# Lookahead and roots in the second attention layer, and a shared comparison in the first, of a graph and expert kernel

## The reference

```python
def _gat(x, src, dst, W, a_src, a_dst, b, heads, ch, concat):
    h = (x @ W).reshape(n, heads, ch)
    es, ed = (h * a_src).sum(-1), (h * a_dst).sum(-1)
    e = jax.nn.leaky_relu(es[src] + ed[dst], SLOPE)
    w = jnp.exp(e - jax.ops.segment_max(e, dst, num_segments=n)[dst])
    alpha = w / jax.ops.segment_sum(w, dst, num_segments=n)[dst]
    return jax.ops.segment_sum(h[src] * alpha[:, :, None], dst, num_segments=n) ... + b

x = x + gat2(relu(layernorm(gat1(layernorm(x)))))
x = x + experts(layernorm(x))     # router, top 2 of 8, gelu between two products
```

## Time and profile before

| | |
|---|---|
| time of three runs | 1572.95, 1572.9 and 1552.66 us |
| median | 1572.9 us |
| profiled execution | 1562.67 us |
| its span (first to last instruction) | 1560.7 us, granted TensorE clock 0.92 on the mean |
| busy in the span | PE 81%, PEld 61%, DVE 59%, ACT 46%, POOL 44% |

### The profile page before, as it was taken

How to read it: one execution, slowest core, us unless ns; L and a number is a source line. 1 busy time by engine, 2 the same in 40 slices (tenths; PEclk the granted TensorE clock), 3 DMA queues, 4 the chain that set the end, 5 groups by cost and what they waited for, 6 DMA issues and landing times.

```text
span 1560.7 us, 21436 instructions
## 1 busy us (share of the span) xinstructions
PE 1259.3 (81%) x6282; PEld 959.0 (61%) x6283; DVE 915.4 (59%) x2551; ACT 725.5 (46%) x1834; POOL 692.8 (44%) x626
## 2 busy tenths in 40 slices
PE   0767798979889989749778788873699999999990
PEld 0545354535445545337567577652699999999980
DVE  6769898999899987525555665667511111111115
ACT  0357665657656667425444544442034344335330
POOL 3600788656666671056565666520422222222220
PEclk9979899999999999869898999886699999999995
DMA  7012633623633470243443554422022222121116
GB/s 223 5 42 78 166 91 89 179 75 89 176 87 89 125 198 25 96 126 102 150 144 103 155 158 113 136 56 78 11 91 94 94 94 91 37 94 37 36 31 250
DMA packets 120379, 160.59 MB, mean 103 GB/s; under 512 B 53198, under 2 KB 93009, under 8 KB 120302
## 3 DMA queue, kind: packets, MB, share of 16 engines
q0 software_dynamic: 28384, 76.23, 17.9%
q1 hardware_dynamic: 86608, 78.89, 16.2%
q10 hardware_dynamic: 5310, 4.58, 0.9%
HBM read 124.98 MB, written 34.64 MB: 102 GB/s over the span
## 4 chain that ended last, share of the span: by engine, by line
PE 50%; DVE 26%; issue 8%; ACT 5%; DMA 4%; another core or an unknown queue 4%; ACTq 1%; SPq 1%; POOL 1%; DVEq 0%; POOLq 0%
PE bank L1381 13%; PE bank L1389 12%; PE bank L1263 9%; PE bank L1214 6%; DVE ring_a L1805 5%; PE bank L1335 4%; DVE ohk L1546 3%; ACT ring_a L1062 2%; DVE ohs L1543 2%; DVE st L1468 2%; PE bank L1123 1%; PE bank L1146 1%; DVE hit L1710 1%; PE bank L1246 1%
## 5 line engine op out<-in xcount | busy, mean ns | idle before, releaser
L750 POOL DMA_INDIRECT arena<-rows,idx_e x385 | 432.8, 1124 | 291.7 <-PE bank L1214 106.4
L1263 PE MATMUL bank<-ring_a,slots 128*65 128x384 f32 (+1 forms) x1000 | 343.9, 457 | 51.7 <-DVE ring_a L1805 45.0
L1335 PE MATMUL bank<-h2t,ring_a 128*128 128x257 f32 x650 | 186.2, 425 | 82.3 <-DVE ring_a L1880 59.3
L982 ACT ACTIVATE ring_a<-vbb,slots 128x384 f32<-128x384 f32 (+1 forms) x500 | 243.8, 562 | 15.4 <-DMA vbb<-v_rows 12.2
L1263 PEld LDWEIGHTS bank<-ring_a,slots 128*65 128x65 f32 x1000 | 136.1, 142 | 181.8 <-issue 101.2
L1805 DVE SCALAR_TENSOR_TENSOR ring_a<-ring_a,arena 128x1536 f32<-128x1536 f32 (+1 forms) x125 | 192.3, 1540 | 16.4 <-ACT ring_a L982 10.3
L1086 ACT ACTIVATE ring_a<-bank,cols 128x128 f32<-128x128 f32 x432 | 128.2, 370 | 158.0 <-PE bank L1381 157.2
L1335 PEld LDWEIGHTS bank<-h2t,ring_a 128*128 128x128 f32 x650 | 126.9, 207 | 116.3 <-DVE ring_a L1880 68.4
L1214 PE MATMUL bank<-arena,ring_a 128*128 128x257 f32 (+1 forms) x770 | 194.3, 402 | 0.0
L1214 PEld LDWEIGHTS bank<-arena,ring_a 128*128 128x128 f32 x770 | 157.4, 205 | 34.9 <-issue 5.4
L1880 DVE SCALAR_TENSOR_TENSOR ring_a<-ring_a,p,arena 128x256 f32<-128x256 f32 (+1 forms) x175 | 79.3, 464 | 114.9 <-ACT ring_a L1062 84.4
(11 more groups left out here) (277 smaller groups left out, 1721.9 us busy)
## 6 DMA issues: line engine op xcount, KB each, us to landing
counts_all<-arena SPq DMA_DIRECT2D x13, 800.0 KB
arena<-counts_all SPq DMA_DIRECT2D x13, 800.0 KB
arena<-in_L_ffn_W SPq DMA_DIRECT2D x8, 1024.0 KB, 7.5
arena<-rows,idx_e POOLq DMA_INDIRECT x385
arena<-ytab SPq DMA_DIRECT2D x4, 1280.0 KB, 11.0
XB<-general_sums SPq DMA_DIRECT2D x38, 130.0 KB
vbb<-in_L_ffn_W SPq DMA_DIRECT2D x4, 1024.0 KB
spare<-in_L_ffn_W SPq DMA_DIRECT2D x4, 1024.0 KB
```

The source lines that it names most:

```text
L750: pool.indirect_dma_start(to[:, k, 0:width], None, table, bass.IndirectOffsetOnAxis(idx_e[:, m * PAIR + k:m * PAIR + k + 1], 0)).then_inc( ...
L982: ins = act.activation(S1[q % SLOTS1][:, h * k * P:(h + 1) * k * P].rearrange("p (t n) -> p t n", n=P), vb1[:, 0:k, h, :], ACT.Copy, scale ...
L1263: pe.matmul(bank[h][0:CH + 1, 0:w_], slots[:, s, h * (CH + 1):(h + 1) * (CH + 1)], S1[q % SLOTS1][:, h * w_:(h + 1) * w_], start=(s == 0), ...
L1335: ins = pe.matmul(bank[(j % 2) * 2 + i][:, 0:W2T], S2[q2 % SLOTS2][:, i * P:(i + 1) * P], h2t[:, s, 0:W2T], start=(s == 0), stop=(s == NT ...
```

## The change

Layer 2, order: ScalarE and VectorE no longer do a step's product just ahead of the same step's other work. ScalarE's loop issues product m and then the other work of step m - 4 (`AHEAD_ACT`), VectorE's loop product m and then the other work of step m - 2 (`AHEAD_DVE`). TensorE, GpSimd and SyncE have the same order by step numbers.

Layer 2, roots: `root_of`, `ask_root` and `refine` are no longer called. `inverse_root` computes the inverse square root on VectorE from the bits of the number and three rounds of Newton, twice in a row for a group, all of it in the step of the group's last `norm`; `turn` comes earlier in the plan by 4 steps for a single tile standing alone.

Layer 1: the comparison is made once for all heads, 128x160 where it was 128x640, and laid out with the five edges innermost; the weights `W1` are laid out head, destination, edge, so that one broadcast over the heads serves. VectorE reads the exponentials of the gathered rows with edges innermost (neighbours 264 numbers apart), and TensorE's weight loads of a pair read every fifth number. In layer 2 the last product of a pair reads the comparison at every fifth number (line 1751).

```diff
+AHEAD_ACT, AHEAD_DVE = 4, 2
@@ plan2
-        g.root = g.norm[-1] + 1
-        g.refine = g.root + 1
+        g.refine = g.norm[-1]
...
-            turn = max(turn + 2, g.refine + 3)
+            turn = max(turn + 2, g.refine + 1)
@@ build
-        hit = sb("hit", [P, PAIR * HEADS * PW])
+        hit = sb("hit", [P, PW, PAIR])
@@ block.scalar
-                for k in range(2):
-                    for g in G2:
-                        if g.root + 2 * k == q:
-                            root_of(slice_of(g), ROOTS2[id(g), k])
...
+            for m in range(END2 + AHEAD_ACT):
+                if m < Q2:
...
                     act.activation(S2[m % SLOTS2][:, 0:k * P], vb2[j % 2][:, 0:k * P], ACT.Relu,
                                    scale=pu2[:, s, 0:1], bias=np2[:, s, 0:1]).then_inc(s_r, 1)
+                q2 = m - AHEAD_ACT
+                if q2 - 1 in ROWS_AT:
+                    rows_out(ROWS_OF[q2 - 1])
+                for p in PAIR2_AT.get(q2 + 2, ()):
+                    exponents(p)
                 hooks2(q2)
@@ block.tensor
-                pair(p, W1T, lambda k: W1[p % 2][:, k, :], bank_of(("pair", p)), True, True)
+                pair(p, W1T, lambda k: W1[p % 2][:, :, :, k].rearrange("p h d -> p (h d)"), bank_of(("pair", p)), True, True)
@@ block.vector
+            def inverse_root(tiles, var):
+                y, y_i = rstd[:, tiles], rstd[:, tiles].bitcast(i32)
+                link(v.tensor_scalar(vpe[:, tiles], var, EPS, None, ALU.add))
+                link(v.tensor_scalar(y_i, vpe[:, tiles].bitcast(i32), 1, None, ALU.arith_shift_right))
+                link(v.tensor_scalar(y_i, y_i, -1.0, float(0x5F3759DF), ALU.mult, ALU.add))
+                for _ in range(3):
+                    link(v.tensor_tensor(tmp_c[:, tiles], y, y, ALU.mult))
+                    link(v.scalar_tensor_tensor(tmp_c[:, tiles], tmp_c[:, tiles], -0.5, vpe[:, tiles], ALU.mult, ALU.mult))
+                    link(v.scalar_tensor_tensor(y, tmp_c[:, tiles], 1.5, y, ALU.add, ALU.mult))
...
-                v.tensor_tensor(w, w, o, ALU.mult).then_inc(s_pw, 1)
+                v.tensor_tensor(w, w, o[:, :, :].rearrange("p d e -> p e d"), ALU.mult).then_inc(s_pw, 1)
...
-            for j, (t0, k) in enumerate(B2):
-                for s in range(NT):
+            for m in range(END2 + AHEAD_DVE):
+                if m < Q2:
...
-                    for p in PAIR2_AT.get(q2 + 1, ()):
-                        pair_weights2(p)
-                    hooks2(q2)
-            for q2 in range(Q2, END2):
+                q2 = m - AHEAD_DVE
+                for p in PAIR2_AT.get(q2 + 1, ()):
+                    pair_weights2(p)
                 hooks2(q2)
```

More of the change, by code:

```diff
@@ L111 @@
 PAIR1_AT, PAIR2_AT = at_step(PAIR1), at_step(PAIR2)
-USES = [("window", w) for w in windows_of(0)]
+USES = [("window", w) for t in range(B1[0][0], B1[0][0] + B1[0][1]) for w in windows_of(t)]
 for _q in range(Q1):
@@ L178 @@
 ROOT1 = {id(g): n for n, g in enumerate(sorted(G1, key=lambda g: g.root))}
-ROOTS2 = {(id(g), k): 4 + len(G1) + n + 1 for n, (_, g, k) in
-          enumerate(sorted(((g.root + 2 * k, g, k) for g in G2 for k in range(2)), key=lambda a: (a[0], a[2], G2.index(a[1]))))}
 END1 = max(g.turn[-1] for g in G1) + 8
@@ L376, in build @@
         S2 = [ring_a[:, k * 256:(k + 1) * 256] for k in range(SLOTS2)]
-        W1 = [ring_a[:, W_AT + k * W_PAIR:W_AT + (k + 1) * W_PAIR].rearrange("p (e c) -> p e c", c=P) for k in range(2)]
+        W1 = [ring_a[:, W_AT + k * W_PAIR:W_AT + (k + 1) * W_PAIR].rearrange("p (h d e) -> p h d e", h=HEADS, d=PW) for k in range(2)]
         W2 = [ring_a[:, W2_AT + k * W_PAIR:W2_AT + (k + 1) * W_PAIR].rearrange("p (e c) -> p e c", c=P) for k in range(P // PW)]
@@ L1063, in _ @@
                                    scale=pu2[:, s, 0:1], bias=np2[:, s, 0:1]).then_inc(s_r, 1)
-                    if q2 - 1 in ROWS_AT:
-                        rows_out(ROWS_OF[q2 - 1])
-                    for p in PAIR2_AT.get(q2 + 2, ()):
-                        exponents(p)
-                    hooks2(q2)
-                    q2 += 1
-            while q2 < END2:
+                q2 = m - AHEAD_ACT
[3 more added lines that the diff above has]
+                    exponents(p)
                 hooks2(q2)
-                q2 += 1
             act.wait_ge(s_gx, 1)
@@ L1719, in pair_weights1 @@
                     v.wait_ge(s_lk, 2)
-                o = hits(p, HEADS)
+                o = hits(p)
                 g, s_in, there = slot_of(p)
@@ L1844, in hooks2 @@
                     row_stats(lambda _: slots[:, t, 0:D], [t])
-                order = sorted(G2, key=lambda g: ROOTS2[id(g), 0])
-                for g in order:
-                    if g.norm[-1] == q:
-                        ask_root(slice_of(g))
-                for g in order:
+                for g in G2:
                     tiles = slice_of(g)
                     if g.refine == q:
-                        refine(tiles, ROOTS2[id(g), 0])
+                        inverse_root(tiles, mv[:, tiles, 1])
                         v.tensor_copy(rs1[:, tiles], rstd[:, tiles])
@@ L1855, in hooks2 @@
                         link(v.tensor_tensor(tmp_b[:, tiles], tmp_b[:, tiles], rstd[:, tiles], ALU.mult))
-                        link(v.tensor_scalar(vpe[:, tiles], tmp_b[:, tiles], EPS, None, ALU.add))
-                        v.sem_inc(s_var, 1)
-                    if g.refine + 2 == q:
-                        refine(tiles, ROOTS2[id(g), 1])
+                        inverse_root(tiles, tmp_b[:, tiles])
                         v.tensor_tensor(rt2[:, tiles], vpe[:, tiles], rstd[:, tiles], ALU.mult)
```

37 lines of the change are left out of this document (17 added, 20 removed).

## The result

Twenty executions of each kernel on one chip gave 1561.12 us before (1552.66 to 1576.84) and **1576.84 us after** (1570.17 to 1586.19), a ratio of 1.0097, 95% interval 1.0069 to 1.0124. The profiled execution of after took 1582.34 us (span 1580.7, clock 0.909). I had forecast 1518 in 1490 to 1570: the sign was wrong and the range missed. None of the three signs of being wrong that I had named showed: the unknown waits didn't grow, VectorE was busy for 65% of layer 2, and a pair's ten instructions in layer 1 kept their time.

A forecast was written before the change was run, and what follows sets the result against it. VectorE paces layer 1; in layer 2 nobody is full and TensorE waits for products while VectorE or ScalarE does step-end work. 1562.7 - 45 (layer 2) + 2 (last tile) - 2 (layer 1) gives 1518 us, range 1490 to 1570.

The forecast's parts named there:

- three signs of being wrong: Unknown waits growing, VectorE passing 90% in layer 2, or a pair's ten layer 1 instructions taking clearly over 2.17 us.
- the lead's -53: Layer 2: products issued two steps ahead on VectorE take up to 53 us of TensorE's idle time.
- the loads' -18: Layer 2: ScalarE's table loads go, with 18 us of them on the path; bounds nothing to 47.
- the clock's -17: Layer 2: the 48 us lost to the lower clock fall with idle time to 31.
- the forecast 56: Layer 2: TensorE's remaining idle time in us, 86 - 53 - 18 + 41.
- my first rival: Layer 2: GpSimd's dense gathers make waits grow, stage not much under 325 us; -15 in all, 1548 us, chance 0.22.
- Longer chains, +41: Layer 2: 12 more rows of 0.19 us on VectorE in each of 18 groups, taken as wholly uncovered.
- my slower rival: Layer 2: VectorE away 8 us per group, 18 groups costing TensorE 6.3 us each; 1607 us, chance 0.08.
- The late signals: Layer 2: waits from dense gathers grow as others shrink; -15 in all, 1548 us, chance 0.22.
- -2 us said: Layer 1: a shorter comparison against a slower spaced read on VectorE, between -23 and +6 us.
- The rival of the weights' spaced read: Layer 1: TensorE's weight load takes 0.33 us and sticks out 460 times, +52 us; 1569 us, chance 0.08.
- The last tile: End of layer 2: the last tile's uncovered chain on VectorE goes from 3.6 to 5.5 us, +2 us.

The follow-up runs named there:

- lead alone: The kernel before with ScalarE's product four and VectorE's two steps ahead, roots on ScalarE; 0.9885, on a slower chip 0.9838, with plain transfers 0.9602.
- plain transfers: Layer 2's gathers from the fifth pair on replaced by plain transfers of neighbouring rows; before 1500.4 us, after 1527.5, split 1484.2, lead alone 1440.0.
- split: The kernel after with the root chain cut in three pieces and the turn five steps behind refine; 0.9972, again 0.9973, with plain transfers 0.9889.

## Why the prediction was wrong

**The step that failed is the lead's -53**, and with it the two gains counted beside it, the loads' -18 and the clock's -17. The lead's term was worked out as "up to 53", at most 1.74 us from each of 42 idle pieces, and it stands in the sum at that upper end. On chips of the kind that the forecast was made on, TensorE's idle time in layer 2 was 83 us before, 60 with the lead alone and 91 after (the lead alone ran on a second such chip). So the lead took 23 us of it where the sum has 53, and the roots with all that belongs to them brought 31 where it has -18 + 41 = 23. Of the 35 us by which idle time missed the forecast 56, the lead makes 30. The clock's term hung on the idle time and fell with it: for the 1300 products TensorE was busy 310 us before, 306 with the lead alone and 313 after.

**What bounds layer 2.** That TensorE waits for a product because VectorE or ScalarE stands at step-end work was right. But what the lead takes from these waits isn't all won, because others stood behind them. In time it gains 301.8 - 264.9 = 37 us with plain transfers, 17 with gathers where signals are on time, and 25 where they are late (0.0162 x 1566). With gathers and signals on time VectorE's wait for ScalarE's product fell from 69.8 to 4.4 us, and a wait of 38.5 us for gathered rows stood in its place, with GpSimd at one gather after the other: the floor of my first rival, which I had near 325 us and which is 316. Where signals are late, these took a further 52 us of the lead alone's layer 2 (368.2 less 316.1). And the table loads stood in the same waits for ScalarE, so the lead covers them too: the sum counted two gains for one wait. With the clock it had 88 us of gains where the lead alone, which keeps the loads, shows 17 to 25.

**Longer chains, +41.** The term priced the 12 added rows of a group as wholly uncovered, and they were: split and lead alone with plain transfers say so, 44 us (some 5 of them the spaced read in a pair's last product). What it left out is that the change also closes up the steps. Ask, first refine and second refine stood in separate steps with products between, and now norm, 29 rows and xn stand in one; with plain transfers that makes 28 us more. In time the roots cost net 72 us with plain transfers, 51 with gathers and the lead, 61 without the lead, and on chips with late signals 41 (1.0097 - 0.9838, two chips). By my terms it is -18 + 41 + 2 = 25, and 38 with 13 more for the clock in proportion to 23 us of idle time. That 38 lies near 41 is luck: it credits loads that gave nothing, leaves out the long piece, and knows nothing of the late signals that hid part of the cost.

**The long chain was my slower rival**, with a chance of 0.08 and 1607 us. Its mechanism is in the trace: 76 of the 91 us of idle time lie in the 18 stretches with the roots. Its price was 6.3 us for each, and they measure 4.2 on the mean. Against it I held that TensorE has some four steps in hand, nearer 6 us, and that was about right, with 5.3 us on the mean; it wasn't enough, because such a stretch, which I had at 8 us, lasts 9.3 us on the mean once VectorE's own waits in it are counted. At which instruction TensorE then waits depends on where the turn is planned; the loss doesn't, as the runs with a later turn say.

**The clock.** I expected 0.92 from less idle time and it was 0.85: idle time rose. The direction of the coupling held (0.96 with 32 us idle, 0.93 with 42, 0.88 with 63, 0.87 with 83, on the chips without late signals).

**The late signals** (rival, 1548). They are real, they belong to dense gathers, and the trace before came from a chip that has them. Between the two kinds of chip layer 2 differs by 61 us in the kernel before (394.0 less 332.7), 52 with the lead alone (368.2 less 316.1) and 40 in after (404.7 less 364.3), so the roots' loss is partly hidden there, and 1.0226 becomes 1.0097. How it is hidden is an inference: TensorE stands waiting for VectorE when a signal would be late, and the gathers, held up by TensorE, are less dense. The share of unknown waits, 15.7% to 4.0%, and the signals on time, 72 of 230 with the lead alone beside 92 and 95, fit it; no run isolates it.

**Table loads and busy times.** ScalarE is busy 126.81 us in layer 2 (I said 125) and VectorE 261.73 (265); no table load is left in its steps. Right, and of no help: with the lead ScalarE's time held nothing back any more, and what VectorE had to do more came back in full.

**Layer 1.** The comparison takes 316 ns (318 said) and the product with the spaced exponentials 1306 ns (1.27 us said): (1306 - 815) / 640 = 0.77 ns a number more. The pair's last product in layer 2, a spaced read of the comparison, went from 327 to 450 ns, 0.77 a number too. The two changes of layer 1 cancel, -2 us said, +1.7 measured with an interval that holds zero (0.9997 to 1.0023). The rival of the weights' spaced read had the load near its bad end, 0.302 us against 0.190, but not the consequence: products still start 0.220 us apart. A recorded load of 0.302 us fits beside a product every 0.220, so that length isn't what must stay under the interval. The Trainium skill (SBUF — State Buffer, Door 1: The DMA port swizzle) says that reads at a step of more than four fp32 numbers pay at each read, and reads at a step of up to four do not; these three rows agree with that, and the runs show that on TensorE it cost hardly any time here, 460 times 1 or 2 ns. The reduction of the earlier trace rows has a step of exactly four, and by my estimate it paid 0.7 ns a number all the same, against the second half of that rule; no run settles this.

**The last tile** (+2): what follows the last product took 489.5 us before and 492.3 after on one kind of chip, +2.8, but the lead alone, which keeps ScalarE's roots, had 492.5, so this isn't told from scatter.

## What to carry to other kernels

When a lead or another overlap is to cover waits, its gain isn't the sum of what it could cover in each: ask what waits next behind them (here the gathers), and count two savings in the same wait once. When work moves onto the engine that feeds the bottleneck, its added time may come back in full (here 44 us), and the longest stretch in which it makes nothing for the bottleneck costs on top (here 28). What isn't in the lead (here a pair's weights) still waits behind the stretch. The lead without the roots is the version to keep: 0.9885 and 0.9838 on the two kinds of chip, against 1.0226 and 1.0097 for the change as made, and a deeper lead of 6 and 4 gives no more (0.9913 beside 0.9838 on chips of one kind).

## What I had not expected of the hardware

The same kernel takes 1500 us on some chips and 1561 to 1568 on others, with 61 us of it in one stage (394.0 and 332.7). On the slower ones TensorE's signals are held, mostly for up to 5 us, at the longest for 12 in the trace before and 14 in that of after, while GpSimd runs one gather of 0.95 us after the other, and then come 0.04 us apart; with plain transfers issued by the same engine they are on time on the same chip. Why only some chips do it stays open.
